# Bilinear sampling of a deformable convolution: five base values and sixteen clipped steps instead of twenty-one cell weights

## The chip, the cores and the metric

One core of one Trainium2 chip. The metric is the device time of one execution in microseconds, smaller is better. The kernel is written with explicit semaphores: every engine runs its own list of instructions in order and waits where the list says so.

## The reference, cut to what matters

Input x is (8, 64, 16, 16). Two residual layers follow each other, each on a group-normalised input. The first is a deformable attention: a 3x3 convolution gives, for each of 8 heads and 9 taps, an offset (dx, dy) and a weight; the values v are sampled bilinearly at the displaced place and summed over the taps.

```python
offsets = conv2d(x, off_w, off_b); aw = sigmoid(conv2d(x, attn_w, attn_b))
xp = (gx + 1.0) * 0.5 * (W - 1); yp = (gy + 1.0) * 0.5 * (H - 1)    # base grid + offset
x0 = floor(xp); y0 = floor(yp); x1 = x0 + 1; y1 = y0 + 1
sampled = corner(y0, x0, wy0*wx0) + corner(y0, x1, wy0*wx1) + corner(y1, x0, wy1*wx0) + corner(y1, x1, wy1*wx1)
head_out = einsum('nhckxy,nhkxy->nhcxy', sampled, aw)                # 9 taps
x = x + einsum('oc,nchw->nohw', Wo, combined)
```

The second layer (two 3x3 branches with running maxima, a 3x3 convolution of their sum, a 1x1 branch, two group norms, a last 3x3 convolution) is the same in both kernels.

## The kernel before

**The sampling as a window.** Instead of gathering, the kernel takes all cells of a window around each point. A partition is one (row y, image n) pair, 128 in all; the free axis runs over tap k, column x and head h. For a displacement d in cells the hat max(0, 1 - |u - d|) is the bilinear weight. Rows dy = -1, 0, 1 have five cells in x (d = -2 to 2), rows dy = -2 and 2 have three, 21 together (`DX`, `CELL0`, `CELLS`). A test (`vmin`, `vfar_sum`, `window_test`) looks whether any displacement leaves the window; a slow path, not taken with these inputs, covers that.

**Chunks.** The 16 columns go through in five chunks of 2, 4, 4, 4 and 2 columns (`CHUNKS`). For each chunk:

- TensorE makes the offsets, one column at a time: `conv_column`, 15 tap matmuls and one for the bias (L982, L990, L992).
- ScalarE copies them to `u` (`copy_offsets`), makes the modulation `mod` (L467), five distances |u - d| for x and y at once (L471, `distances`) and turns them to hats (L481, `hats`).
- VectorE makes `wy` = y hat times modulation (L777), a window check `edge`, then five products `prod` = x hat times `wy`, one for each row (L742), and sums the three cells of its own row over the nine taps by itself (L794, `cell`).
- TensorE sums the other 18 cells over the taps by nine transposes accumulated in PSUM, in three groups (`tap_sum`, L1009; 5 blocks of up to 128 columns in a chunk of four columns, 3 in a chunk of two); ScalarE copies each group back (`copy_sums`, L489) and TensorE transposes it again (`cells_back`, L1022).
- VectorE multiplies the weights with the shifted values, five `apply` instructions (L769) into a ring of three buffers `part` (`PARTS`); TensorE sums them by transposes (`row_sum`, L1034) and so frees a buffer (`part_used`). ScalarE evacuates (`evacuate`), TensorE projects (`y0`, L1045), VectorE adds the residual of the chunk before (`residual`, L688) between two applies.

Some `conv_column`s of later chunks stand on TensorE between these steps, by hand: `BEFORE` = (0, 1, 2, 0, 0) ahead of `tap_sum`, `BETWEEN` = (3, 2, 2, 0, 0) one ahead of each of the first `row_sum`s. Warm-up matmuls on constants stand ahead of `tap_sum` of chunks 3 and 4 (`WARM_CHUNK`).

**The start.** VectorE and ScalarE spread the normalised image and split it in a rounded and a rest part, in three ranges of columns (`RANGES`): VectorE casts to `g_pair` (L718) and subtracts to `g_cross` (L720); ScalarE copies both to the upper partitions (`copy_high`, L429 and L430). Chunk 0's convolution needs range 0 alone. ScalarE does `copy_high(2)` ahead of `copy_offsets(0)`. TensorE does chunk 0, two columns of chunk 1, then the values (`values`, 32 matmuls, L959, which need all three ranges), then the rest of chunk 1. GpSimd clears `wp_s` (L388) as soon as `w_split` is 2, which VectorE's L724 gives.

**The shifted values.** ScalarE copies the values from PSUM to `v[:, WIN]` (L441), and four DMAs on SP's queue shift them by -2, -1, 1 and 2 rows into the other rows of `v` (L327), in the order in which the applies use them.

Of the kernel before, what the change touches and what calls it, by code (L numbers as in the profile page):

```python
# [27 lines left out]
ALU = mybir.AluOpType  # L28
# [8 lines left out]
K2 = KS * KS  # L37
# [64 lines left out]
def build(nc, x, consts, w_off, w_v, off_bias, w_o, w12, b12, wp, wc1, wc2, vecs, out):  # L102
    with ExitStack() as ctx:
# [9 lines left out]
        x_t = sb("x_t", [C, N, HW])  # L113
# [10 lines left out]
        beyond = sb("beyond", [P, 2 * CKM])  # L124
        hat = sb("hat", [P, 2, ND, 2 * CKM])
        wy = sb("wy", [P, ND, CKM])
        prod = sb("prod", [P, CELLS * CKM])
        cell_t = sb("cell_t", [P, 5, P])
        cell = sb("cell", [P, 3, CXM])
        v = sb("v", [P, ND, W + 2 * WIN, C])  # L130
# [12 lines left out]

        vfar = part[:, :, :, :].rearrange("p b d s -> p (b d s)")[:, 0:VW * C].rearrange("p (x c) -> p x c", c=C)
# [35 lines left out]
        r12 = x_t[:, 0:HALF, :].rearrange("p (b r) q -> p b r q", b=2)  # L180
        maxima = x_t[:, HALF:N, :].rearrange("p (b r) q -> p b r q", b=2)
# [40 lines left out]
        v_moved = [sem(f"v_moved{i}") for i in range(ND)]  # L222
        off_ps = sem("off_ps")
# [5 lines left out]
        hat_used = sem("hat_used")  # L229
# [60 lines left out]
        def cell_blocks(c, g):  # L290
            q0, q1, _ = GROUPS[g]
            cols = (q1 - q0) * CHUNKS[c][1] * HEADS
            n = -(-cols // P)
            return n, cols // n, 2 * g, bank[(2, 3, 2)[g]]

        def cells_ps(c, i):
            cx = CHUNKS[c][1] * HEADS
            if CELL0[i] >= GROUPS[-1][0]:
                return bank[3][:, 2 * P:2 * P + 3 * cx]
            return cell_bank[:, CELL0[i] * cx:(CELL0[i] + 5) * cx]  # L300
# [8 lines left out]
        def _(sp):  # L309
# [13 lines left out]
            sp.wait_ge(v_ready, 1)  # L323
            for i in (4, 1, 3, 0):
                d = (i - WIN) * N
                dst, src = (slice(0, P - d), slice(d, P)) if d > 0 else (slice(-d, P), slice(0, P + d))
                sp.dma_start(v[dst, i, WIN:WIN + W, :], v[src, WIN, WIN:WIN + W, :]).then_inc(v_moved[i], 16)  # L327
# [14 lines left out]
            with sp.If(count > 0):  # L342
# [6 lines left out]
                             v[:, WIN, WIN:WIN + W, :].rearrange("p x c -> p (x c)")).then_inc(far_v0, 16)  # L349
# [13 lines left out]
        def _(pool):  # L363
# [44 lines left out]
        def _(act):  # L408
# [28 lines left out]
            def copy_values():  # L437
                act.wait_ge(v_zero, 1)
                act.wait_ge(v_ps, 1)
                for b in range(4):  # L440
                    last = nc.scalar.activation(v[:, WIN, WIN + 4 * b:WIN + 4 * (b + 1), :],  # L441
                                                bank[4 + b][:, :].rearrange("p (x q) -> p x q", q=P)[:, :, 0:C],
                                                ACT.Copy)
                last.then_inc(v_ready, 1)
# [16 lines left out]
            def distances(c, d0, d1):  # L461
                x0, w = CHUNKS[c]
                ck = K2 * w * HEADS
                xs = slice(x0, x0 + w)
                act.wait_ge(u_ready, c + 1)
                if d0 == 0:
                    nc.scalar.activation(mod[:, :, xs, :], u[:, 2 * K2:, xs, :], ACT.Sigmoid).then_inc(mod_ready, 1)  # L467
                    if c >= 2:
                        act.wait_ge(hat_used, c - 1)
                for d in range(d0, d1):  # L470
                    nc.scalar.activation(  # L471
                        hat[:, c % 2, d, 0:2 * ck].rearrange("p (k x h) -> p k x h", x=w, h=HEADS),
                        u[:, 0:2 * K2, xs, :], ACT.Abs, bias=float(WIN - d), scale=STEP).then_inc(dist_done, 1)

            def hats(c):
# [749 lines left out]
```

## Time and profile before

| | us |
|---|---|
| median of 3 runs | 151.67 |
| lowest, highest | 150.72, 152.64 |
| span of the profiled execution | 149.2 |
| start-up to the first VectorE work of chunk 1 | 0 to 43.84 |
| chunks 1 to 4 and the last residual | 43.84 to 109.51 |
| second layer and the output | 109.51 to 149.2 |

The profile has a page (busy time of the engines, the span in 40 slices, the chain of work that ended last, groups of instructions) and a trace that can be asked for stretches. "busy" of a matmul is modelled and overlaps its neighbours, so for TensorE the distance from start to start is what counts. A record's length on VectorE or ScalarE overlaps the next one by some 0.08 us.

### The profile page before, as it was taken

To read this page: it belongs to the slowest core of one execution; us is meant where nothing else is said; L and a number is where in the kernel's file an instruction comes from. 1 tells how busy PE (TensorE), PEld (TensorE's weight loads), DVE (VectorE), ACT (ScalarE), POOL (GpSimd) and SP (SyncE) were. 2 spreads that over 40 slices of the span, in tenths; PEclk is the share of its full clock that TensorE was granted. 3 is DMA by queue.
4 is the path that set the end of the run, shared out by engine and by line. 5 is a ranking of instruction groups with operands and counts; after the bars stand their busy time and mean duration, and the time that the engine had idled before them with its cause. 6 is when DMAs were issued, how large, how long until landed. Compare 5 with 4: busy or idle time off the path is not lost.

```text
span 149.2 us, 3269 instructions
## 1 busy us (share of the span) xinstructions
PE 129.2 (87%) x1395; PEld 111.3 (75%) x1395; DVE 110.5 (74%) x198; ACT 57.4 (38%) x102; POOL 18.5 (12%) x27
## 2 busy tenths in 40 slices
PE   4966399999999899999999998899887999797790
PEld 3654399998898889999899896687655667465460
DVE  5429895095459999799998999998757297965701
ACT  3009539837950768007880128012030317021100
POOL 8941120000000000000018000000003001030100
PEclk9999659999999999999999999999999999999999
DMA  3980000009964000000000000000000000000033
GB/s 95 271 152 0 0 0 4 0 15 256 244 120 108 19 7 0 0 0 4 0 0 0 0 4 0 0 0 4 0 2 4 4 0 4 0 4 0 0 75 70
DMA packets 6672, 5.48 MB, mean 37 GB/s; under 512 B 4656, under 2 KB 5938, under 8 KB 6658
## 3 DMA queue, kind: packets, MB, share of 16 engines
q1 hardware_dynamic: 5986, 4.26, 12.0%
q10 hardware_dynamic: 672, 1.02, 2.7%
q8 instruction: 11, 0.18, 0.5%
q14 instruction: 3, 0.02, 0.1%
HBM read 2.85 MB, written 0.52 MB: 23 GB/s over the span
## 4 chain that ended last, share of the span: by engine, by line
PE 50%; DVE 25%; issue 9%; DMA 6%; ACT 5%; SPq 1%; POOL 1%; POOLq 0%; DVEq 0%
PE bank L990 10%; PE bank L1009 9%; PE bank L982 8%; PE bank L1034 7%; DVE prod L742 7%; DMA prod<-in_w_off 6%; DVE part L769 3%; DVE x_t L861 3%; PE bank L1164 3%; PE bank L1131 3%; PE bank L959 2%; DVE wy L777 2%; DVE pooled L867 2%; DVE bn L580 2%; PE bank L943 2%
## 5 line engine op out<-in xcount | busy, mean ns | idle before, releaser
L742 DVE TENSOR_TENSOR prod<-hat,wy 128x1440 f32<-128x1440 f32 (+3 forms) x25 | 27.3, 1159 | 0.0
L769 DVE TENSOR_TENSOR part<-v,bank 128x1280 f32<-128x1280 f32 (+3 forms) x20 | 21.7, 1109 | 7.1 <-PE bank L1034 3.5
L1009 PE MATMUL bank<-cst,prod 128*128 128x128 f32 (+3 forms) x189 | 22.3, 272 | 0.8 <-DVE prod L742 0.8
L1034 PE MATMUL bank<-cst,part 128*128 128x128 f32 x168 | 21.1, 274 | 1.8 <-DVE part L769 1.4
L1009 PEld LDWEIGHTS bank<-cst,prod 128*128 128x128 f32 (+3 forms) x189 | 20.7, 131 | 1.4 <-DVE prod L742 1.0
L1034 PEld LDWEIGHTS bank<-cst,part 128*128 128x128 f32 x168 | 18.3, 140 | 3.2 <-DVE part L769 3.0
L943 PE MATMUL bank<-ones_r 128*128 128x512 f32 x67 | 18.5, 428 | 2.1 <-POOL w_pair L370 2.1
L990 PE MATMUL bank<-w_cross,g_cross 128*128 128x216 f32 x144 | 19.9, 285 | 0.0
L990 PEld LDWEIGHTS bank<-w_cross,g_cross 128*128 128x128 f32 x144 | 18.6, 203 | 0.0
L982 PE MATMUL bank<-w_pair,g_pair 128*128 128x216 f32 x96 | 15.3, 301 | 3.7 <-ACT g_cross L430 3.7
L943 PEld LDWEIGHTS bank<-ones_r 128*128 128x128 f32 x67 | 13.3, 207 | 4.9 <-POOL w_pair L370 2.1
L982 PEld LDWEIGHTS bank<-w_pair,g_pair 128*128 128x128 f32 x96 | 13.1, 209 | 4.4 <-issue 4.3
L471 ACT ACTIVATE hat<-u 128x576 f32<-128x576 f32 (+1 forms) x25 | 13.7, 579 | 0.0
L377 POOL TENSOR_TENSOR ab<-ab,half_pow 128x2 f32<-128x2 f32 (+1 forms) x7 | 5.8, 834 | 55.7 <-DVE ab L604 53.5
L481 ACT ACTIVATE hat<-hat 128x2880 f32<-128x2880 f32 (+1 forms) x5 | 10.7, 2132 | 0.2
L777 DVE TENSOR_TENSOR wy<-hat,mod 128x1440 f32<-128x1440 f32 (+1 forms) x5 | 6.8, 1351 | 5.2 <-ACT hat L481 5.2
L489 ACT ACTIVATE cell_t<-bank 128x256 f32<-128x256 f32 (+5 forms) x15 | 4.7, 317 | 14.4 <-PE bank L1009 14.3
L1164 PE MATMUL bank<-g,wc_s 64*64 64x256 f32 x144 | 8.5, 379 | 2.0 <-DVE g L890 2.0
L456 ACT ACTIVATE u<-bank 128x432 f32<-128x432 f32 x7 | 3.4, 528 | 16.3 <-PE bank L992 16.3
L1151 PE MATMUL bank<-pooled,wp_s 64*64 64x256 f32 x144 | 8.6, 379 | 1.1 <-DVE pooled L867 1.1
L1164 PEld LDWEIGHTS bank<-g,wc_s 64*64 64x64 f32 x144 | 5.9, 132 | 4.2 <-ACT g L547 2.9
L1131 PE MATMUL bank<-g,w_s 64*32 64x256 f32 x288 | 8.5, 377 | 0.1
(101 smaller groups left out, 154.9 us busy)
## 6 DMA issues: line engine op xcount, KB each, us to landing
v<-v SPq DMA_DIRECT2D x2, 480.0 KB, 6.2
v<-v SPq DMA_DIRECT2D x2, 448.0 KB, 5.9
prod<-in_w_off ACTq DMA_DIRECT2D x1, 486.0 KB, 7.0
prod<-in_w_off SPq DMA_DIRECT2D x1, 486.0 KB, 8.8
w_s<-in_w SPq DMA_DIRECT2D x4, 72.0 KB, 4.4
wc_s<-in_wc SPq DMA_DIRECT2D x2, 144.0 KB, 3.4
wp_s<-in_wp SPq DMA_DIRECT2D x4, 72.0 KB, 2.5
x_b<-in_x SPq DMA_DIRECT2D x1, 256.0 KB, 4.9
```

Of the source, the lines that this page charges most:

```text
L471: nc.scalar.activation(hat[:, c % 2, d, 0:2 * ck].rearrange("p (k x h) -> p k x h", x=w, h=HEADS), u[:, 0:2 * K2, xs, :], ACT.Abs, bias=fl ...
L481: nc.scalar.activation(hat[:, c % 2, :, 0:2 * ck], hat[:, c % 2, :, 0:2 * ck], ACT.Relu, bias=1.0, scale=-1.0).then_inc(hat_ready, 1)
L742: return nc.vector.tensor_tensor(prod[:, 0:K2 * CELLS * cx].rearrange("p (k q s) -> p q k s", k=K2, s=cx)[:, q0:q0 + nd], hat[:, c % 2, d0 ...
L769: nc.vector.tensor_tensor(part[:, n % PARTS, 0:nd, 0:cv].rearrange("p d (q e) -> p d q e", e=HD), moved, weights.unsqueeze(3).to_broadcast ...
L777: made_wy = tick(nc.vector.tensor_tensor(wy[:, :, 0:ck].rearrange("p d (k q) -> p d k q", k=K2), hat[:, c % 2, :, ck:2 * ck].rearrange("p ...
L943: nc.tensor.matmul(ps.rearrange("p (a q) -> p a q", q=P), ones_r[:, :], ones_r[:, :].unsqueeze(1).to_broadcast([P, 4, P]), start=True, sto ...
L982: nc.tensor.matmul(column_ps(c, j), g_pair[:, x + 2 * single, ky:ky + H, :].rearrange("p y n -> p (y n)"), w_pair[:, t, :], start=(t == 0) ...
L990: nc.tensor.matmul(column_ps(c, j), g_cross[:, x + kx, ky:ky + H, :].rearrange("p y n -> p (y n)"), w_cross[:, t, :], start=False, stop=False)
L1009: last = nc.tensor.matmul(out_ps[0:size, b * P:(b + 1) * P], prod[:, at:at + size], ident, start=(b == 0 and t == 0), stop=(b == n - 1 and ...
L1034: last = nc.tensor.matmul(comb_bank[:, j * P:(j + 1) * P], part[:, n % PARTS, d, j * P:(j + 1) * P], ident, start=(m == 0 and d == 0 and j ...
L1131: last = nc.tensor.matmul(image(bank[R12_BANK[g] + r][cols, 0:HW]), w12_s[rows, t, b * CD:(b + 1) * CD], window(g1, rows, DUO * g + k, t), ...
L1164: last = nc.tensor.matmul(image(bank[OUT_BANK[g] + k][r * C:(r + 1) * C, 0:HW]), wc2_s[rows, t, :], window(g2, rows, DUO * g + r, t), star ...
```

## The change

For one row the hats h(-2) .. h(2) in x sum to one inside the window, so the sum over five cells of h(d) v(d) is written as v(-2) plus four clipped steps min(1, max(0, u - d)) times the column differences v(d+1) - v(d), d = -2 .. 1. In rows dy = -2 and 2 the base is v(-1) and there are two steps. In numbers for a chunk:

- The five y hats times modulation are the weights of the bases. They are written into `prod` (places 16 to 20) and not into `wy`, and VectorE sums all five over the taps (before: three cells).
- 16 products step times base (4, 4, 4, 2, 2 cells), before 21.
- TensorE's `tap_sum` has two groups of 8 cells, before 8, 7 and 3: in a chunk of four columns 4 blocks and not 5, in one of two columns 2 and not 3. `cells_back` and `copy_sums` follow.
- The applies: one with the five bases, then rows of 4, 4, 4 terms, then rows 3 and 4 (2 terms each) as two instructions into one buffer. 21 terms as before. The order of rows is dy = 0, -1, 1, -2, 2.
- ScalarE: one |u| for both axes (`dist`), four row distances, four clipped ramps in x, each with their second step; 13 instructions for a chunk and not 7, on as many elements. `copy_sums` stands at two places and not three.
- A new tensor `dv` of column differences: GpSimd clears it (5 x 19 x 64 elements, ahead of the clearing of `wp_s`), later subtracts in two pieces when the values are there, and SP shifts it by rows in two pieces of 8 and 9 columns, eight DMAs behind the four of `v` and ahead of the second layer's weights. The four of `v` carry 14 or 15 columns, not 16.
- The first apply of chunk 0 waits for all four shifted rows of `v`; the steps of chunk 0 for `dv`'s first piece, row by row.
- TensorE makes the values directly behind chunk 0, then all four columns of chunk 1. `y0(c - 1)` stands ahead of the last `cells_back`.
- `x_t` is gone; its later use lies in `v`.

The diff, cut to its core:

```diff
-DX = [1, 2, 2, 2, 1]
-GROUPS = ((0, 8, 2), (8, 15, 3), (15, 18, 4))
+STEPS_X = ((-2, 4), (-2, 4), (-2, 4), (-1, 2), (-1, 2))
+GROUPS = ((0, 8, 2), (8, 16, 5))
+TERMS = (5, 4, 4, 4, 4)
+VCOLS = W + 3
+D_PIECES = ((1, 9), (9, 18))
...
+        dv = sb("dv", [P, ND, VCOLS, C])
...
+            sp.wait_ge(v_ready, 4)
+            for i in range(1, ND):
+                dst, src = row_parts(i)
+                at = -BASES[i]
+                sp.dma_start(v[dst, i, at:W, :], v[src, 0, 2:2 + W - at, :]).then_inc(v_moved[i], 16)
+            sp.wait_ge(dv_zero, 1)
+            for k, (xa, xb) in enumerate(D_PIECES):
+                sp.wait_ge(dv_ready, k + 1)
+                for i in range(1, ND):
+                    dst, src = row_parts(i)
+                    sp.dma_start(dv[dst, i, xa:xb, :], dv[src, 0, xa:xb, :]).then_inc(dv_moved[k][i], 16)
...
             pool.wait_ge(w_split, 2)
+            nc.gpsimd.memset(dv[:, :, :, :], 0.0).then_inc(dv_zero, 1)
             nc.gpsimd.memset(wp_s[:, :, :, :], 0.0).then_inc(wp_zero, 1)
+            pool.wait_ge(v_zero, 1)
+            pool.wait_ge(dv_zero, 1)
+            for k, (xa, xb) in enumerate(((0, 9), (9, 18))):
+                pool.wait_ge(v_ready, 2 * (k + 1))
+                nc.gpsimd.tensor_tensor(dv[:, 0, xa:xb, :], v[:, 0, xa + 1:xb + 1, :], v[:, 0, xa:xb, :],
+                                        ALU.subtract).then_inc(dv_ready, 1)
...
             copy_high(2)
             copy_offsets(0)
-            distances(0, 0, ND)
-            hats(0)
+            sizes_and_modulation(0)
+            row_distances(0)
+            row_hats(0)
+            short_of(0)
+            steps_x(0)
             copy_values()
...
+                copy_sums(c, 0)
                 if c + 1 < NC:
-                    distances(c + 1, ND - 1, ND)
-                    hats(c + 1)
+                    row_distances(c + 1)
+                copy_sums(c, 1)
+                if c + 1 < NC:
+                    row_hats(c + 1)
+                    short_of(c + 1)
+                    steps_x(c + 1)
...
-                for i in ROWS[:-1]:
+                ve.wait_ge(hat_ready, 2 * c + 2)
+                for i in range(ND):
                     product(i).then_inc(prod_ready, 1)
...
+                base_sum = tick(nc.vector.tensor_reduce(
+                    cell[:, :, 0:cx], cells[:, bases].rearrange("p q k s -> p q s k"), AX_X, ALU.add))
+                apply_bases()
+                apply_steps((0,))
+                apply_steps((1,))
+                if c:
+                    residual(c - 1)
+                apply_steps((2,))
...
+                apply_steps((3, 4))
...
-            conv_column(1, 0)
-            conv_column(1, 1)
             values()
-            conv_column(1, 2)
-            conv_column(1, 3)
-            pe.wait_ge(v_ready, 1)
+            for j in range(CHUNKS[1][1]):
+                conv_column(1, j)
+            pe.wait_ge(v_ready, 4)
...
                 cells_back(c, 0)
-                tap_sum(c, 2)
-                cells_back(c, 1)
-                cells_back(c, 2)
                 if c:
                     y0(c - 1)
+                cells_back(c, 1)
```

## Rows read from the trace of the kernel before

**Rows 1.** Busy time by stretch: chunks 1, 2, 3, then 4 to last residual (start:end, length, engines)
```profile
43.84:61.80 17.96, 16.98 (x156) 16.43 (x156) 16.76 (x18) 8.74 (x15) 0.00 (x0) 1.00 0.14 32
61.80:79.90 18.10, 17.93 (x166) 17.46 (x165) 16.98 (x17) 9.27 (x16) 1.88 (x4) 1.00 0.00 1
79.90:96.92 17.02, 15.79 (x125) 13.90 (x124) 16.88 (x17) 5.24 (x13) 1.57 (x2) 1.00 0.00 1
96.92:109.51 12.59, 11.22 (x93) 9.31 (x92) 10.23 (x23) 1.48 (x5) 0.00 (x0) 1.00 0.01 2
```

**Rows 2.** Waits over the whole span: who for whom, total us, times, longest
```profile
DVE part L769 <- PE bank L1034: 3.5, 3, 1.5
```

**Rows 3.** Groups by form, VectorE: busy us, mean ns of one, idle before
```profile
L742 DVE TENSOR_TENSOR prod<-hat,wy 128x1440 f32<-128x1440 f32 x9 | 14.4, 1653 | 0.0
L769 DVE TENSOR_TENSOR part<-v,bank 128x1280 f32<-128x1280 f32 x9 | 13.1, 1479 | 0.0
...
L794 DVE TENSOR_REDUCE cell<-prod 128x96 f32<-128x864 f32 x3 | 5.1, 1694 | 0.1
...
L769 DVE TENSOR_TENSOR part<-v,bank 128x768 f32<-128x768 f32 x3 | 2.9, 950 | 2.0 <-PE bank L1034 2.0
...
L794 DVE TENSOR_REDUCE cell<-prod 128x48 f32<-128x432 f32 x2 | 1.8, 901 | 0.0
```

**Rows 4.** Timeline of TensorE in chunk 1: tap sums (start, us, xcount)
```profile
49.07 4.17 PE L1009 MATMUL bank<-cst,prod 128*128 128x128 f32 x36 [0.81 <-DVE prod L742]
```

**Rows 5.** The chain that ended last: chunk 0's end, the values, a column of the convolution
```profile
23.63 0.11 PE bank L992
...
27.31 3.53 PE bank L959 x32
...
65.51 0.67 PE bank L982 x6
66.18 1.01 PE bank L990 x9
```

**Rows 6.** Timeline of all engines, 15 to 26 us: casts, memset, what ScalarE waits for
```profile
15.28 0.53 DVE L718 CAST g_pair<-g_t 64x720 fp32r<-64x720 f32 x1 [0.47 <-ACT g_t L423]
...
19.44 1.40 DVE L718 CAST g_pair<-g_t 64x576 fp32r<-64x576 f32 x1
19.47 1.06 POOL L388 MEMSET wp_s<- 128x1152 f32 x1 [3.04 <-DVE w_cross L724]
...
21.55 0.82 DVE L718 CAST g_pair<-g_t 64x1296 fp32r<-64x1296 f32 x1
...
22.40 1.28 ACT L429 ACTIVATE g_pair<-g_pair 64x1296 fp32r<-64x1296 f32 x1 [0.28 <-DVE g_pair L718]
...
24.89 0.59 ACT L451 ACTIVATE u<-bank 128x216 f32<-128x216 f32 x2
```

**Rows 7.** Timeline of GpSimd: the clearing of v
```profile
1.99 5.44 POOL L371 MEMSET v<- 128x6400 f32 x1
```

**Rows 8.** Granted clock by stretches of 1 us (value ahead of the last two columns)
```profile
15.00:16.00 1.00, 0.00 (x0) 0.00 (x0) 0.69 (x2) 0.79 (x3) 0.20 (x1) 0.92 0.00 0
...
22.00:23.00 1.00, 1.00 (x8) 1.00 (x7) 0.97 (x2) 0.72 (x2) 0.00 (x0) 0.67 0.00 0
```

**Rows 9.** Timeline of TensorE: its first work behind the idle stretch
```profile
17.45 2.87 PE L982 MATMUL bank<-w_pair,g_pair 128*128 128x216 f32 x12 [3.75 <-ACT g_cross L430]
```

**Rows 10.** Timeline of ScalarE: distances and hats of chunk 0, the copies of the values
```profile
25.74 1.76 ACT L471 ACTIVATE hat<-u 128x288 f32<-128x288 f32 x5
...
28.10 1.41 ACT L481 ACTIVATE hat<-hat 128x1440 f32<-128x1440 f32 x1
30.94 1.22 ACT L441 ACTIVATE v<-bank 128x256 f32<-128x256 f32 x4 [1.43 <-PE bank L959]
```

**Rows 11.** The tile v: its four DMAs, ns to issue, first and last start; landing
```profile
L327 SPq DMA_DIRECT2D v<-v x4: 593/876/2054, 32.2 to 34.7; - x4
...
DMA to landing us min/median/max: 3.7/6.2/8.1
```

More of the change, by code:

```diff
@@ L222, in build @@
         v_moved = [sem(f"v_moved{i}") for i in range(ND)]
+        dv_zero = sem("dv_zero")
+        dv_ready = sem("dv_ready")
+        dv_moved = [[sem(f"dv_moved{i}_{k}") for i in range(ND)] for k in range(len(D_PIECES))]
         off_ps = sem("off_ps")
@@ L464, in distances, with sizes_and_modulation @@
+            def sizes_and_modulation(c):
+                x0, w = CHUNKS[c]
                 xs = slice(x0, x0 + w)
                 act.wait_ge(u_ready, c + 1)
[L466 to L473, printed above, removed]
@@ new lines, in sizes_and_modulation, with row_distances, short_of @@
+                if c >= 2:
+                    act.wait_ge(prod_ready, ND * (c - 1))
+            def row_distances(c):
+                for i in range(1, ND):
+                    nc.scalar.activation(functions(c, 1, i), displacement(c, 1), ACT.Abs, bias=-float(DYS[i]),
+                                         scale=STEP).then_inc(dist_done, 1)
+            def short_of(c):
+                for i in range(1, ND):
+                    nc.scalar.activation(functions(c, 0, i), displacement(c, 0), ACT.Relu, bias=float(i - 2),
+                                         scale=-STEP).then_inc(dist_done, 1)
@@ new lines, in apply_bases, with apply_steps @@
+                def apply_bases():
+                    if c == 0:
+                        ve.wait_ge(v_ready, 4)
+                        for i in range(1, ND):
+                            ve.wait_ge(v_moved[i], 16)
+                    to = next_part()
+                    ve.wait_ge(step, base_sum)
+                    weighted(to, v, 0, x0, ND, VCOLS * C, cell[:, :, 0:cx]).then_inc(part_ready, 1)
+                def apply_steps(rows):
+                    to = next_part()
+                    d = 0
+                    for i in rows:
+                        if c == 0 and i == 0:
+                            ve.wait_ge(dv_ready, len(D_PIECES))
+                        if i and c in (0, 2):
+                            ve.wait_ge(dv_moved[c // 2][i], 16)
+                        ve.wait_ge(cell_ps, len(GROUPS) * c + (1 if STEP0[i] < GROUPS[0][1] else 2))
+                        at, n = STEPS_X[i]
+                        last = weighted(to[:, d:d + n], dv, i, x0 + at + 2, n, C,
+                                        cells_ps(c, i).rearrange("p (d q) -> p d q", d=n))
+                        d += n
+                    last.then_inc(part_ready, 1)
@@ L798, in chunk @@
-                for m, i in enumerate(APPLY[:-1]):
-                    if c and m == ND - 2:
-                        residual(c - 1)
-                    apply(i)
+                base_sum = tick(nc.vector.tensor_reduce(
[6 more added lines that the diff above has]
+                apply_steps((2,))
```

163 lines of the change are left out of this document (75 added, 88 removed).

## The prediction

> **What bounds the kernel now.** I read first the busy time of the engines by stretch, cut where VectorE begins a chunk. In chunks 1 to 3 VectorE is busy 16.8, 17.0 and 16.9 us of 18.0, 18.1 and 17.0, and TensorE is as full in the first two [rows 1]. So neither alone sets the pace. The waits say how the two are tied: VectorE's idle time in an apply ends with a row sum, 3.5 us in three waits [rows 2]; the last apply of a chunk needs one of the three buffers back, and TensorE has convolution columns between the row sums. Then I read the lengths of single instructions: VectorE's by form [rows 3], TensorE's from its timeline and from the chain [rows 4, 5]. Last, because the change puts new work there, the start: the timelines of all engines from 15 to 26 us [rows 6], the granted clock and the DMAs that shift the values. There no engine is full; the chain goes through whoever is late.
>
> **The steady chunks: what they gain.** VectorE's products cost 1.653 us for 1440 elements (5 cells of 288) [rows 3] and follow each other 0.08 closer than their records. I take 1.04 ns an element, the slope between the two forms of the applies being alike: (1.479 - 0.950)/512 = 1.03 [rows 3]. 21 cells are 6.7 us in the trace's chunk, 16 cells 4608 x 1.04 = 4.8 plus 5 starts of 0.07, 5.15: 1.55 less. The sum over the taps grows from 3 cells to 5: 1.694 us for 864 elements and 0.901 for 432 [rows 3] make 1.84 ns an element, so 1440 cost 2.75, 1.05 more. The applies have the same 21 terms and one instruction more, 0.1. The base product writes as much as `wy` did; into the strided `prod`, as the products have always done. Net 0.4 less on VectorE, 16.9 to 16.5 or 16.7 with its small gaps. The reduction is the trap in the title: of the 1.55 saved, two thirds are given back.
>
> TensorE loses 9 of 45 tap transposes; 36 take 4.17 us with the tail of the last [rows 4], 0.11 each, so 1.0 less, one block of `cells_back` (0.1) and one handover through ScalarE (0.3) less. Row sums stay, transposes of the same shape and price; a column of the convolution is 0.67 + 1.01 + 0.11 for the bias = 1.8 [rows 5].
>
> The period is a loop over both: products ready; second tap sum 2.0; cells back and `y0` 0.8; column 1.8, row sum 1.1, column 1.8, row sum 0.9 (now a buffer is free); last apply 1.3; base product and check 2.0, products 5.15. Sum 16.85. VectorE's own sum is 16.7, so the loop sets it by little. Against 17.96 and 18.10 [rows 1] that gives 1.1 and 1.25 us. In chunk 3 no columns stand between, VectorE sets the end: 17.02 to 16.65, 0.4. Chunks 1 to 3 together: 2.75 less. In chunk 4, 9 of 27 transposes go (1.0), VectorE's products lose 0.8 and the reduction adds 0.5; from its start to the last residual 12.59 [rows 1] becomes 11.65, 0.95 less. Steady part: **3.7 us less**.
>
> **The start: what the new clearing does.** GpSimd now clears `dv` at the moment at which it cleared `wp_s`, 19.47. `dv` has 6080 elements; `v` with 6400 took 5.44 us [rows 7], `wp_s` with 1152 took 1.06 [rows 6], so 0.83 ns an element and 5.17 us: 19.47 to 24.65. Beside it VectorE casts range 1 and range 2 of `g_pair`. The cast of 720 elements took 0.53 and that of 1296 took 0.82, without GpSimd; the one of 576, by that 0.45, took 1.40 and ended at 20.84, 0.3 behind the memset that ran beside it [rows 6]. So a cast does not run beside a memset of GpSimd; it stood for about the whole 0.95 that was left of it. I take the same with the long one: the cast of range 1 begins at 24.6 and ends at 25.0. Then GpSimd's `wp_s` runs and the cast of range 2 waits for it to 26.05 and ends at 26.8, before 22.37. If GpSimd's two memsets follow without a gap it is 27.6; if VectorE wins the first race, range 2 alone waits and ends at 25.9. Bounds of the delay: 3.5 to 5.2, I take 4.5, for it is the order that the trace shows.
>
> The Trainium skill, page "SBUF — State Buffer", section on the shared port, says that VectorE in a two-port mode (casts and copies) and GpSimd hold a common pair of ports exclusively, the loser standing for the whole instruction. The trace shows that for 1.06 us [rows 6] and can't show it for 5.17. By the page the delay is whole; if a wait were never longer than the 0.95 seen, it would be nothing beyond what is there, and that is my first rival.
>
> Who waits: ScalarE's `copy_high(2)` began at 22.40, on the cast, and `copy_offsets(0)` stands behind it, at 24.89 [rows 6]. Both move by 4.5: offsets copied from 29.35. Chunk 0's convolution is done at 23.7 [rows 5] and is not touched. But the values now stand directly behind it, and need `copy_high(2)`: TensorE has nothing from 23.7 to 29.35, 5.6 us, where before it had two columns of chunk 1 (3.6 us) as cover. The cover is gone.
>
> **The clock.** TensorE resumed at 17.45 from an idle time of 3.75 [rows 9], so it had worked to 13.7; the granted clock was 0.92 in the stretch 15 to 16 and 0.5 behind it [rows 8]: it fell to the lower level 2.2 us into the idle time. It came back at 22.3 (0.67 in 22 to 23), 4.9 us after the work resumed at 17.45; a matmul took 0.24 (12 in 2.87) [rows 9] where it takes 0.11 (6 in 0.67) [rows 5]. I expect the same for an idle time of 5.6: lower level at 26, and the values from 29.35 half as fast. They took 3.53 us [rows 5]; now 22 of 32 at 0.22 and 10 at 0.11, to 35.35.
>
> **ScalarE and the values.** Distances of 288 elements follow each other by 0.34 (5 in 1.76), the hats' 1440 elements took 1.41 [rows 10]. The new order, by these: |u| 0.35, four row distances of 144 elements 0.9, row hats 1.0, hence bases' weights ready 3.2 behind the offsets' start (before, all at 4.6); four ramps 0.9 and their second step 0.7, done at 4.75. Then the check 0.6: ScalarE is free at 34.7, so 0.7 before the values are. Copies 1.22 [rows 10]: `v_ready` at 36.65, before 32.16.
>
> **The DMAs.** The first shift landed 3.7 us behind its issue, at 35.9, the last at 34.7 + 8.1 = 42.8 [rows 11]: three of them, 1408 KB, in 6.9 us, 204 KB/us. Now v is 4 x 420 KB: first 40.3, last 46.5, and the first piece of `dv`, 928 KB, by 51.0. The bases wait for all of v, 46.5 to 47.3; rows 0 to 2 to 49.4. GpSimd's subtractions (576 elements each; from a memset's 0.6 to a few us) lie between 36 and 46 and are hidden either way.
>
> **Chunk 0 on TensorE.** Columns of chunk 1 4 x 1.8 to 42.5; tap sums to 44.5; ScalarE has `u` of chunk 1, |u|, and four row distances (1.5) ahead of the second copy: cells back at 46.6 (that is 1.3 us of waiting which no form of before has). Column, row sum, column, row sum: 51.2. Only then is the buffer for rows 3 and 4 free; `dv` is there too. Two short applies, 0.8: VectorE starts chunk 1 at **52.0**, before 43.84: 8.2 later.
>
> **Sum.** +8.2 - 2.75 - 0.95 = **+4.5 us**. The second layer is unchanged, and so is what lies outside the span. The profiled execution has 149.2, so 153.7; the runs' median is 2.5 above it, so 151.67 + 4.5 = **156.2 us**, 3.0% slower.
>
> **Rivals.** (1) *No blocking* (or one of under 1 us): the steady gain wins. Then the values start at 24.9, `v_ready` 31.45, and VectorE starts chunk 1 at 45.0 (buffers) to 46.2 (`dv` landing at 45.8): 1.2 to 2.4 later, minus 3.7, is -1.3 to -2.5: 149.8 us, at the best 149.2. What decides is the length of the cast of range 1 or 2: under 1.5 us, this one. Against it stands the one long cast [rows 6]. (2) *Blocked, but the clock does not fall* in the idle time: values 2.4 earlier on TensorE, row sums of chunk 0 2.5 earlier, VectorE at 49.5: +2.0, 153.7 us. For it: nothing in the trace; against it [rows 8]. (3) *Blocked twice or DMAs slower*: the two memsets in one go (+0.7), the lower clock lasting into chunk 1's columns (up to +1.5) or `dv` rows late behind each other: 157.5 to 158.5. (4) *A real gain of over 2%*: rival 1 with the shifted rows of `dv` landing at the pace of the first transfer and VectorE's steady period down to its own 16.5: 148.3.
>
> **Chances.** Forecast 0.60, rival 1 0.12, rival 2 0.12, rival 3 0.11, rival 4 0.05. The forecast's own terms (4.5 by 3.5 to 5.2; half-speed time by a microsecond; period by 0.2 a chunk) spread it from 154.8 to 157.3. The range leaves out rivals 1 and 4 and the top of 3: 152.3 to 158.0. A measurement of this kernel tells about 2%, 3.0 us, from no change: slower is the forecast but its low edge, rival 3, and a little of 2: 0.68; within 2% 0.25; faster 0.07.
>
> **What would show it.** Right: a cast of `g_pair` of 4 to 6 us beside GpSimd's `dv` memset; TensorE idle from 23.7 to about 29; a granted clock of 0.5 there; VectorE's base product of chunk 1 at 52; chunk starts 16.8 apart; reductions of 2.75 and 16 cells in 5.2. Wrong: casts of under 1 us (rival 1), clock 1.0 throughout (rival 2), a wait of VectorE for the `dv` DMA that ends behind 51, or chunk starts still 18 apart.

## The result and the profile after

| | before | after |
|---|---|---|
| median, us | 151.39 (4 runs) | 159.98 (4 runs) |
| lowest, highest | 150.72, 152.64 | 159.81, 161.34 |
| span of the profiled execution | 149.2 | 157.9 |
| mean granted clock of it | 0.976 | 0.934 |

The ratio is 1.060, 95% interval 1.051 to 1.068: 8.6 us slower where 4.5 was forecast, and the time lies above the range.

The start-up, on all engines between 20 and 31 us, after (start, duration, engine, line, operation, what the engine waited for):

```profile
20.00 5.50 DVE L774 CAST g_pair<-g_t 64x576 fp32r<-64x576 f32 x1
20.03 5.17 POOL L408 MEMSET dv<- 128x6080 f32 x1 [3.03 <-DVE w_cross L780]
25.13 1.37 POOL L409 MEMSET wp_s<- 128x1152 f32 x1
...
26.21 0.97 DVE L774 CAST g_pair<-g_t 64x1296 fp32r<-64x1296 f32 x1
...
29.70 0.59 ACT L477 ACTIVATE u<-bank 128x216 f32<-128x216 f32 x2
29.82 0.45 PE L1028 MATMUL bank<-w_v_pair,g_pair 128*128 128x128 f32 x1 [4.96 <-ACT g_cross L457]
```

The cast of 576 elements takes 5.50 us where it took 1.40 [rows 6]; it is over 0.3 behind the clearing of `dv`. `copy_offsets(0)` starts 4.8 later than before [rows 6], and TensorE stands idle for 4.96 us ahead of the values. (The cast itself begins 0.56 later in this execution, behind a load that landed later.)

The clock in those stretches (sum of the stretch, busy time of each engine, granted clock, DMA share, GB/s), after:

```profile
26.00:27.00 1.00, 0.00 (x0) 0.00 (x0) 1.00 (x2) 0.79 (x2) 0.50 (x1) 1.00 0.00 0
27.00:28.00 1.00, 0.00 (x0) 0.00 (x0) 0.96 (x2) 0.78 (x1) 0.00 (x0) 0.90 0.00 0
28.00:30.00 2.00, 0.18 (x1) 0.21 (x2) 1.15 (x4) 1.98 (x4) 0.00 (x0) 0.50 0.00 0
30.00:40.00 10.00, 10.00 (x48) 10.00 (x49) 5.29 (x9) 5.99 (x21) 2.20 (x2) 0.50 0.03 7
40.00:41.00 1.00, 1.00 (x6) 1.00 (x6) 0.00 (x0) 0.00 (x0) 0.58 (x1) 0.50 0.94 172
41.00:42.00 1.00, 1.00 (x9) 1.00 (x8) 0.00 (x0) 0.00 (x0) 0.00 (x0) 0.77 0.93 298
```

It fell in the idle time as expected, 2.9 us into it, but it was back at full speed only at 41.5: 11.6 us after TensorE had resumed, with TensorE full all the while. All the values, the first column of chunk 1 and part of the second ran at half speed. The low stretch ahead of it lasted longer too: from the idle time before chunk 0's convolution the clock was back at 24.4, 6.4 us after the work resumed at 18.02 (before: 22.7, 5.2 us), and chunk 0's convolution ended at 24.9 and not at 23.7. TensorE in the columns, after:

```profile
36.68 1.55 PE L1051 MATMUL bank<-w_pair,g_pair 128*128 128x216 f32 x6
38.03 2.12 PE L1059 MATMUL bank<-w_cross,g_cross 128*128 128x216 f32 x9
...
40.16 1.45 PE L1051 MATMUL bank<-w_pair,g_pair 128*128 128x216 f32 x6
...
42.57 0.83 PE L1051 MATMUL bank<-w_pair,g_pair 128*128 128x216 f32 x6
...
46.15 2.02 PE L1078 MATMUL bank<-cst,prod 128*128 128x128 f32 x17
```

The first column takes 3.5 us (36.68 to 40.16), the second 2.4, the others 1.8; the tap sums begin at 46.15.

VectorE from the last work of chunk 0 on, after:

```profile
37.30 1.40 DVE L863 TENSOR_REDUCE cell<-prod 128x80 f32<-128x720 f32 x1
48.46 0.82 DVE L810 TENSOR_TENSOR part<-v,cell 128x640 f32<-128x640 f32 x1 [9.76 <-DMA v<-v]
49.20 1.28 DVE L810 TENSOR_TENSOR part<-dv,bank 128x512 f32<-128x512 f32 x2
52.77 0.69 DVE L810 TENSOR_TENSOR part<-dv,bank 128x512 f32<-128x512 f32 x1 [2.29 <-PE bank L1100]
54.98 0.75 DVE L810 TENSOR_TENSOR part<-dv,bank 128x256 f32<-128x256 f32 x2 [1.53 <-PE bank L1100]
55.65 1.65 DVE L848 TENSOR_TENSOR prod<-hat,mod 128x1440 f32<-128x1440 f32 x1
```

The last line is the start of chunk 1: 55.65, before 43.84 [rows 1], so 11.8 later. The largest wait by far, 9.76 us for the DMA of `v`, looks like the cause; an experiment below shows what it costs.

Between the starts of the chunks, after:

```profile
55.65:72.77 17.12, 16.24 (x149) 15.54 (x148) 16.28 (x19) 8.91 (x20) 0.00 (x0) 1.00 0.24 47
72.77:89.93 17.16, 16.87 (x156) 16.29 (x155) 16.50 (x18) 9.44 (x21) 2.00 (x4) 1.00 0.00 1
89.93:106.38 16.45, 14.62 (x111) 12.35 (x109) 16.35 (x19) 5.40 (x18) 1.46 (x2) 1.00 0.00 1
```

Chunks 1 to 3 take 50.73 us and took 53.08 [rows 1]: the sampling itself is 2.35 us faster, and chunk 4 is some 0.9 faster. So 11.8 - 2.35 - 0.9 = 8.6, which is what the times say (the spans: 8.7).

### The profile page after: what moved, and what is told of

It is laid out like the page before. It is cut to its first block, busy times and chain, and to the rows that moved or that the text cites. A ratio compares the mean times of both kernels' runs of the same rounds, so it can differ in the third digit from the quotient of the medians.

```text
span 157.9 us, 3217 instructions
## 1 busy us (share of the span) xinstructions
PE 131.6 (83%) x1345; PEld 112.5 (71%) x1345; DVE 112.6 (71%) x203; ACT 58.3 (37%) x127; POOL 26.4 (17%) x30
## 3 DMA queue, kind: packets, MB, share of 16 engines
q1 hardware_dynamic: 7038, 6.10, 17.3%
## 4 chain that ended last, share of the span: by engine, by line
PE 40%; DVE 35%; issue 9%; DMA 6%; ACT 6%; SPq 1%; POOL 1%; DVEq 1%; POOLq 0%
DVE prod L802 10%; PE bank L1059 7%; DMA prod<-in_w_off 6%; PE bank L1078 5%; DVE part L810 5%; PE bank L1051 5%; PE bank L1028 4%; DVE g_pair L774 4%; PE bank L1100 4%; DVE v L930 3%; PE bank L1226 3%; PE bank L1193 3%; DVE prod L848 2%; PE bank L1089 2%; DVE pooled L936 1%
## 5 line engine op out<-in xcount | busy, mean ns | idle before, releaser
L810 DVE TENSOR_TENSOR part<-dv,bank 128x512 f32<-128x512 f32 (+2 forms) x25 | 19.9, 832 | 5.1 <-PE bank L1100 5.1
L802 DVE TENSOR_TENSOR prod<-hat,prod 128x576 f32<-128x576 f32 (+2 forms) x25 | 21.3, 920 | 0.5 <-ACT hat L531 0.5
L1012 PE MATMUL bank<-ones_r 128*128 128x512 f32 x67 | 19.3, 443 | 2.2 <-POOL w_pair L390 2.1
L1059 PEld LDWEIGHTS bank<-w_cross,g_cross 128*128 128x128 f32 x144 | 20.2, 218 | 0.0
L1078 PE MATMUL bank<-cst,prod 128*128 128x128 f32 x144 | 17.3, 274 | 1.3 <-DVE prod L802 1.3
L1078 PEld LDWEIGHTS bank<-cst,prod 128*128 128x128 f32 x144 | 15.8, 140 | 2.5 <-DVE prod L802 2.2
L810 DVE TENSOR_TENSOR part<-v,cell 128x1280 f32<-128x1280 f32 (+1 forms) x5 | 6.1, 1225 | 10.2 <-DMA v<-v 9.8
L863 DVE TENSOR_REDUCE cell<-prod 128x160 f32<-128x1440 f32 (+1 forms) x5 | 10.9, 2189 | 0.0
L1028 PE MATMUL bank<-w_v_pair,g_pair 128*128 128x128 f32 x16 | 6.7, 417 | 5.0 <-ACT g_cross L457 5.0
L848 DVE TENSOR_TENSOR prod<-hat,mod 128x1440 f32<-128x1440 f32 (+1 forms) x5 | 6.8, 1353 | 3.7 <-ACT hat L525 3.7
L1028 PEld LDWEIGHTS bank<-w_v_pair,g_pair 128*128 128x128 f32 x16 | 5.3, 331 | 5.1 <-DVE w_v_cross L785 5.1
```

Source lines behind the costliest of these rows:

```text
L802: return nc.vector.tensor_tensor(cells[:, STEP0[i]:STEP0[i] + n], hat[:, c % 2, at + 3:at + 3 + n, 0:ck].rearrange("p d (k s) -> p d k s", ...
L810: return nc.vector.tensor_tensor(to.rearrange("p d (q e) -> p d q e", e=HD), moved, weights.unsqueeze(3).to_broadcast([P, n, cx, HD]), ALU ...
L848: made_bases = tick(nc.vector.tensor_tensor(cells[:, bases], hat[:, c % 2, :, ck:2 * ck].rearrange("p d (k s) -> p d k s", s=cx), mod[:, : ...
L863: base_sum = tick(nc.vector.tensor_reduce(cell[:, :, 0:cx], cells[:, bases].rearrange("p q k s -> p q s k"), AX_X, ALU.add))
L1012: nc.tensor.matmul(ps.rearrange("p (a q) -> p a q", q=P), ones_r[:, :], ones_r[:, :].unsqueeze(1).to_broadcast([P, 4, P]), start=True, sto ...
L1028: last = nc.tensor.matmul(bank[4 + x // 4][:, (x % 4) * P:(x % 4 + 1) * P].rearrange("p (a c) -> p a c", c=C), src[:, x + 1, 1:H + 1, :].r ...
```

## The experiments

The kernels are built on the one after, unless said otherwise. Times are medians; before, on the same chips, was 151.2 to 151.7.

### What the clearing costs

**Cleared late.** `dv` is cleared behind `wp_s`, once VectorE's last split is done.

```diff
-            nc.gpsimd.memset(dv[:, :, :, :], 0.0).then_inc(dv_zero, 1)
             nc.gpsimd.memset(wp_s[:, :, :, :], 0.0).then_inc(wp_zero, 1)
+            pool.wait_ge(w_pair_ready, 3)
+            nc.gpsimd.memset(dv[:, :, :, :], 0.0).then_inc(dv_zero, 1)
```

> The changed kernel with one move on GpSimd: dv is cleared behind wp_s and only when VectorE has given w_pair_ready 3, its last cast of the start. Theory A (the common port: the 5.17 us clearing holds VectorE's cast of range 1, and all that follows from it, the lower clock too, makes the loss): the cast of 576 elements is back at 1.4 us (beside wp_s), TensorE idle between chunk 0 and the values for 1.2 us and not 5, granted clock 1.0 from 23 us on, chunk 1 begins on VectorE at 45.5 to 47, the time is 149.5 to 151.5 us, a ratio to the kernel before of 0.985 to 1.0. Theory B (the loss is of the new order on TensorE and of the twelve shifting DMAs, the clearing is beside it): chunk 1 begins behind 51 and the time stays over 155 us.

154.8 us (153.3 to 155.2), ratio 1.021 (1.014 to 1.027). The casts and the clearings in it:

```profile
19.59 1.40 DVE L775 CAST g_pair<-g_t 64x576 fp32r<-64x576 f32 x1
21.69 0.82 DVE L775 CAST g_pair<-g_t 64x1296 fp32r<-64x1296 f32 x1
...
19.61 1.06 POOL L408 MEMSET wp_s<- 128x1152 f32 x1 [3.04 <-DVE w_cross L781]
24.57 5.17 POOL L410 MEMSET dv<- 128x6080 f32 x1 [3.89 <-DVE w_v_cross L786]
```

The same memset of 5.17 us, moved to where VectorE has no cast, gives back 5.2 us of the 8.6. But 149.5 to 151.5 was expected. The clock was not at 1.0 from 23 us on; by slices of 3.8 us, with VectorE's bases and its start of chunk 1:

```profile
PEclk9999955557999999999999999999999999999999
...
43.33 0.83 DVE L811 TENSOR_TENSOR part<-v,cell 128x640 f32<-128x640 f32 x1 [9.27 <-DMA v<-v]
...
50.78 1.65 DVE L849 TENSOR_TENSOR prod<-hat,mod 128x1440 f32<-128x1440 f32 x1
```

It was at the lower level from 19.3 to 36.4, although TensorE stood idle for only 0.53 and 0.87 us in that time, and the values took 6.9 us here too. So the slow values do not need the idle time of 5 us, and the 5.2 us, between two kernels that both have them, are the price of the blocked cast.

**A clearing put into the kernel before.** GpSimd clears 3840 elements of `part` (for nothing but the time it takes) ahead of `wp_s`; VectorE waits for it behind its last split.

```diff
             pool.wait_ge(w_split, 2)
+            nc.gpsimd.memset(part[:, :, :, :], 0.0).then_inc(extra_clear, 1)
             nc.gpsimd.memset(wp_s[:, :, :, :], 0.0).then_inc(wp_zero, 1)
...
+            ve.wait_ge(extra_clear, 1)
```

> The kernel before, with one clearing more on GpSimd at the place where the changed kernel clears dv: the buffers part, 3840 elements, 3.2 us by 0.83 ns an element (dv itself finds no room in this kernel); VectorE waits for it long after. It computes the same. Theory A (the common port alone): the cast of 576 elements takes 3.6 us and not 1.4, or 4.6 if both clearings go ahead of it; ScalarE's offsets of chunk 0 come 2.2 to 3.2 us later, and the time is 153.5 to 155.5 us, more if the clock stays low behind the idle time that TensorE gets. Theory B: the clearing costs nothing, 151 to 152 us.

154.9 us (152.0 to 155.6; four runs too far apart for an interval).

```profile
20.00 4.63 DVE L720 CAST g_pair<-g_t 64x576 fp32r<-64x576 f32 x1
...
20.03 3.30 POOL L389 MEMSET part<- 128x3840 f32 x1 [3.04 <-DVE w_cross L726]
23.27 1.06 POOL L390 MEMSET wp_s<- 128x1152 f32 x1
```

One cast stands for both memsets back to back, 4.4 us. With none of the new sampling chunk 1 begins 4.5 later (48.36), of which 0.6 was there before the cast began. So a clearing alone makes the start late. Its size in the time is less sure: three runs are 2.7 to 4.1 us above the median before, and one, 151.95, is within 0.4 and has no trace.

### What the order of the values and the clock cost

**Columns ahead of the values**, as before the change.

```diff
+            conv_column(1, 0)
+            conv_column(1, 1)
             values()
-            for j in range(CHUNKS[1][1]):
-                conv_column(1, j)
+            conv_column(1, 2)
+            conv_column(1, 3)
```

> The changed kernel with TensorE's order of before: two columns of chunk 1 stand ahead of the values again, the clearing of dv stays where it is. The columns need range 1 alone, so they can begin at 26.8 and fill the idle time up to the values. Theory A: the cast stays at 5.5 us, ScalarE's offsets stay at 29.7. If the clock falls only in the long idle time, an idle time of 2.1 us keeps it at 1.0, values end at 34, chunk 1 begins at 51 to 52.5, time 155.5 to 157. If it falls here too, all stays at 159 to 160. Theory B's order part alone: the time falls to 152.

160.4 us (159.6 to 162.5), ratio 1.058 (1.052 to 1.063): nothing, in either direction. TensorE's idle time is 2.25 us and not 5, but the values come later by the columns and the bases wait to 48.34. Whether a short idle time keeps the clock up was not tested by it: the clock had fallen at 18.8, ahead of that idle time, and was back at 32.5.

**Both together.**

> The changed kernel with both: dv cleared late and two columns of chunk 1 ahead of the values. Theory A: no idle time of TensorE between 18 and 40 us, clock 1.0, steady gain in full: v is ready later than with the values first (32.2 against 31.5), chunk 1 on VectorE at 45.5 to 47, time 149.5 to 151 us, within 0.7 us of the kernel with the clearing late alone. Theory B: over 153.

154.9 us (153.7 to 156.1), ratio 1.022 (1.015 to 1.029), as with the late clearing alone, although the clock is 1.0 in the values and the columns are done at 35.3 and not at 41.3. The bases still wait for the DMA, to 43.80, TensorE stands idle behind them for 3.4 us, and chunk 1 starts at 50.00. So the lower clock of the late clearing cost nothing while `v` landed this late. Both kernels missed what was expected of them if the blocked cast made the loss, 149.5 to 151.5 us.

**Warm-up products in the gap.** 20 of them (0.23 us each) between chunk 0 and the values; the clearing stays early.

```diff
+            keep_warm(20, bank[0][:, :])
             values()
```

> The changed kernel with 20 warm-up matmuls on constants (4.7 us) in TensorE's idle time behind chunk 0. Nothing is earlier for any other engine; only the clock can differ. Theory A with the clock's part as large as the trace makes it (values 6.9 us instead of 3.5, two columns 3.5 us longer than they should): clock 1.0 from 25 us on, values 29.8 to 33.4, columns of chunk 1 done at 40.6 instead of 46.2, chunk 1 begins at 51 to 52.5 instead of 55.7, time 155.5 to 157 us. If the clock matters nothing on the path (the DMAs of v land as late anyway, at 48): 159 us or more.

Four runs, on two levels: 155.8 and 157.6, and twice 161.9, with a mean clock of 0.978 and 0.967 in the first two and 0.947 in the others. The profiled one is that of 157.6. Its clock by slices, and VectorE's start of chunk 1:

```profile
PEclk9999956999999999999999999999997899999999
...
51.43 1.65 DVE L848 TENSOR_TENSOR prod<-hat,mod 128x1440 f32<-128x1440 f32 x1
```

Here the clock is up in the values, and chunk 1 starts 4.2 earlier than after (51.43, not 55.65), although the cast took 6.50 us, 1.0 longer: in this execution VectorE did not get in between the two memsets. There is a second low stretch this time, between the layers (118.7 to 121.7 us, slice 31 and 32 of the clock row), which costs some of that again. The two runs at 161.9 have no trace.

**Both idle times covered**: 15 more warm-ups ahead of chunk 0, 24 in the gap.

```diff
-WARM_LOAD, WARM_START, WARM_CHUNK = 14, 18, (0, 0, 0, 16, 10)
+WARM_LOAD, WARM_START, WARM_CHUNK = 14, 33, (0, 0, 0, 16, 10)
...
+            keep_warm(24, bank[0][:, :])
             values()
```

> The changed kernel as it is, with 15 more warm-up products ahead of the first convolution and 24 between the convolutions of chunk 0 and the values (0.23 us each at full clock), so that TensorE is never idle for long in the start; the clearing and the transfers stay. If the lower clock behind the blocked cast is worth what one look with 20 warm-ups gave (chunk 1 at 51.4 where the changed kernel has 55.7), the time is 154.5 to 156.5 and the runs lie close together. If the lower clock costs little because the transfers of v end the wait anyway: 159 to 160.

159.9 us (158.3 to 161.5), ratio 1.050 (1.041 to 1.059). I had miscounted the cover: chunk 0 now ended at 22.0, the warm-ups at 27.6, the cast again took 6.5, and 2.6 us of idle time were left. TensorE around it:

```profile
21.98 5.64 PE L1012 MATMUL bank<-ones_r 128*128 128x512 f32 x24
30.24 0.30 PE L1028 MATMUL bank<-w_v_pair,g_pair 128*128 128x128 f32 x1 [2.62 <-ACT g_cross L457]
...
31.05 0.34 PE L1028 MATMUL bank<-w_v_cross,g_cross 128*128 128x128 f32 x1
31.19 0.42 PE L1028 MATMUL bank<-w_v_pair,g_pair 128*128 128x128 f32 x1
```

The clock fell at 31.1, that is 0.9 us after work had resumed, and stayed low for 10.2 us. Chunk 1 starts at 55.41. Against the execution with 20 warm-ups (the same cast of 6.5, the same transfers, the clock up) that is 4.0 us. The kernel after against that execution gives 4.2, plus 1.0 for its shorter cast, less 0.3 for its later start: 4.9. So the lower clock behind the blocked cast costs 4 to 5 us. That comes out of single executions: the covers did not keep the clock up reliably, and the medians of the two covered kernels, 159.7 and 159.9, are that of the kernel after.

### What the transfers of v cost

**The first chunks' part of v alone goes first.** Columns 0 to 5 are shifted at once, the rest behind the first piece of `dv`; chunk 2 waits for it. With late clearing and columns first, as in "both together".

```diff
-                sp.dma_start(v[dst, i, at:W, :], v[src, 0, 2:2 + W - at, :]).then_inc(v_moved[i], 16)
+                sp.dma_start(v[dst, i, at:V_SPLIT, :], v[src, 0, 2:2 + V_SPLIT - at, :]).then_inc(v_moved[i], 16)
...
+                for i in range(1, ND):
+                    if k:
+                        dst, src = row_parts(i)
+                        at = -BASES[i]
+                        sp.dma_start(v[dst, i, V_SPLIT:W, :], v[src, 0, 2 + V_SPLIT - at:2 + W - at, :]).then_inc(v_rest[i], 16)
...
+                    if c == 2:
+                        for i in range(1, ND):
+                            ve.wait_ge(v_rest[i], 16)
```

> The changed kernel with both moves, and v shifted in two pieces as dv is: the columns up to 5, which chunks 0 and 1 need, first (some 520 KB instead of 1680), then dv's first piece, then the rest of v and of dv, for which chunk 2 waits. The bases stay first. Theory C: bases at 39.5 to 40.5, no idle time of TensorE over 1.5 us in chunk 0, dv's first piece by 43.5, chunk 1 begins at 44.8 to 46, time 149.5 to 150.7 us: the steady gain of some 3 us shows for the first time against the kernel before. Theory D: the same bytes and four DMAs more to issue, chunk 1 behind 48, 153 us or more.

**148.8 us** (148.4 to 150.1), ratio 0.983 (0.976 to 0.990): faster than the kernel before, by 1.0 to 2.4%.

```profile
38.42 0.82 DVE L818 TENSOR_TENSOR part<-v,cell 128x640 f32<-128x640 f32 x1 [4.75 <-DMA v<-v]
39.16 1.37 DVE L818 TENSOR_TENSOR part<-dv,bank 128x512 f32<-128x512 f32 x2
41.93 0.69 DVE L818 TENSOR_TENSOR part<-dv,bank 128x512 f32<-128x512 f32 x1 [1.39 <-PE bank L1111]
44.15 0.75 DVE L818 TENSOR_TENSOR part<-dv,bank 128x256 f32<-128x256 f32 x2 [1.53 <-PE bank L1111]
44.82 1.65 DVE L859 TENSOR_TENSOR prod<-hat,mod 128x1440 f32<-128x1440 f32 x1
```

The bases start at 38.42, not 43.80, and chunk 1 5.2 us earlier; 6.1 us by the times. The idle time of TensorE behind the bases, and the low clock that came with it at 45 to 48 us, are gone too. Chunks 1 to 3 take 50.73 us here as in the kernel after, and chunk 4 is 0.8 faster than before; the start is 1.0 later than before (44.82 against 43.84), which leaves the 2.2 us by which the span is shorter.

**The same pieces in the kernel after**, with the early clearing and the values first.

> The changed kernel with v shifted in two pieces, so that chunks 0 and 1 wait for the first only; dv is still cleared early and the values still stand directly behind the convolutions of chunk 0. If the whole-row transfers of v are what bounds the start by themselves, the saving seen between the kernels with whole rows and with pieces (6.1 us) comes here too: about 154. If the clearing and TensorE's lower clock set the end of chunk 0 as well (in the changed kernel columns at 46.3, bases at 48.5, so that the transfers were only about 2 us behind the columns), it saves 2 us at most: 158 to 160. My theory is the second.

160.0 us (159.5 to 161.0), ratio 1.060 (1.054 to 1.066): nothing at all.

```profile
42.95 0.82 DVE L817 TENSOR_TENSOR part<-v,cell 128x640 f32<-128x640 f32 x1 [4.73 <-DMA v<-v]
48.69 1.29 DVE L817 TENSOR_TENSOR part<-dv,bank 128x512 f32<-128x512 f32 x2 [4.92 <-PE bank L1099]
52.45 0.69 DVE L817 TENSOR_TENSOR part<-dv,bank 128x512 f32<-128x512 f32 x1 [2.47 <-PE bank L1110]
54.66 0.75 DVE L817 TENSOR_TENSOR part<-dv,bank 128x256 f32<-128x256 f32 x2 [1.53 <-PE bank L1110]
55.33 1.65 DVE L858 TENSOR_TENSOR prod<-hat,mod 128x1440 f32<-128x1440 f32 x1
```

The wait for the DMA has lost 5 us, and a wait of 4.92 for TensorE's `cells_back` (L1099) stands in its place: the columns, in part at half speed, end at 45.8. The longest wait of the profile after was worth nothing while TensorE was that late, and 6.1 us where the columns were done at 35.3.

**Own row first** (whole rows of `v`, late clearing, columns first): in chunk 0 the steps of row 0, which need no transfer, stand ahead of the bases.

```diff
-                apply_bases()
-                apply_steps((0,))
+                if c:
+                    apply_bases()
+                    apply_steps((0,))
+                else:
+                    apply_steps((0,))
+                    apply_bases()
...
-                w, nd = CHUNKS[c][1], TERMS[m]
+                w, nd = CHUNKS[c][1], (TERMS if c else (4, 5, 4, 4, 4))[m]
```

> The changed kernel with both moves (dv cleared late, two columns of chunk 1 ahead of the values) and one more: in chunk 0 the steps of the own row, which need no DMA, are applied ahead of the bases, which wait for all four shifted rows. In the kernel with both moves the bases came at 43.8, TensorE stood from 41.3 to 44.7 for them and its clock fell. Theory C (what is left of the loss is that wait and the idle time behind it): the first row sum at 41, the clock stays, bases at 43.8 to 44.6, chunk 1 begins at 46.5 to 47.5 and not at 50.0, time 151.0 to 152.5 us. Theory D (the amount of data moved is the limit, the order is nothing): chunk 1 at 49 or later, 154 to 155 us.

153.3 us (151.9 to 158.0, ten runs), ratio 1.011 (1.006 to 1.016). By the medians 1.6 us of the 6.1 come from what is queued behind the waiting bases, by the start of chunk 1 in the two profiled executions (46.91 and 50.00) 3.1 of 5.2; the rest came only with the shorter transfers.

### What is left in the start

**Copy order.** On top of the pieces: in chunk 0 `copy_sums(0, 1)` ahead of the row distances of chunk 1.

```diff
                 copy_sums(c, 0)
+                if c == 0:
+                    copy_sums(c, 1)
                 if c + 1 < NC:
                     row_distances(c + 1)
-                copy_sums(c, 1)
+                if c:
+                    copy_sums(c, 1)
```

> The same as the kernel with v in pieces, and in chunk 0 ScalarE copies the second group of sums ahead of the four row distances of chunk 1 (TensorE waited 1.2 us for that copy in all variants). Expected: cells back 1.2 us earlier, chunk 1 begins 0.5 to 1.2 us earlier if TensorE's row sums set its start, nothing if the last dv row does; 148.5 to 150.5 us.

148.0 us (146.6 to 150.3), ratio 0.973 (0.966 to 0.980). 0.8 by the medians, with overlapping runs: likely, not shown.

**Values first, with pieces and late clearing.**

> The changed kernel with dv cleared late and v in two pieces; unlike the 148.8 us version the values stand directly behind the convolutions of chunk 0, as in the changed kernel. If the short idle of TensorE at 24 us before the values lets the lower clock stay until about 36, as in the run with the late clearing alone, the columns come at 41.4 and chunk 1 starts at about 48 to 50: 151.5 to 154. If the order of the two makes no difference once the transfers are short: 148.8.

151.7 us, and again two levels: 149.0 and 149.6, and 153.8 and 154.5 with a mean clock of 0.944 (the ratio, 0.989 with 0.982 to 0.995, is that of the lower two). The profiled one is of the first (chunk 1 at 45.10). At the upper level the order costs at most 0.8 us against 148.8; why two runs had the lower clock is not shown.

Beside the late clearing alone, which differs only in the whole rows of `v`, this shows what the pieces are worth. At a mean clock of 0.942 to 0.944 the times are 154.7 to 155.2 without pieces and 153.8 and 154.5 with them; at 0.966 it is 153.3 without, and at 0.974 and 0.988 149.0 and 149.6 with them. Slow values and late rows of `v` stand side by side and end at about the same time: with whole rows the clock was worth nothing ("both together"), at the lower clock the pieces are worth about 1 us, and only without both do 4 to 6 us come back. The runs are few, and those at 153.8 and 154.5 have no trace.

**The same with 5 warm-ups** between chunk 0 and the values.

> As the kernel before it in this list, with 5 warm-up products put between the convolutions of chunk 0 and the values, where TensorE stood idle for 0.9 us. If it is the clock in the values that costs the time, the cover brings back 148.5 to 150. If it is the order of values and columns, it stays where the run without the cover is, within 0.5.

150.6 us (149.5 to 151.1), ratio 0.996 (0.991 to 1.002). None of the four runs is at 154; by four runs against two of four that speaks for the clock as the cause, without proving it. Three of them lie 0.8 us and more above the lower two of the kernel without the warm-ups, which is not explained.

**The start covered**: the version with copy order and 15 more warm-ups ahead of chunk 0's convolution.

> The version with pieces and copy order of 148.0 us, with 15 more warm-up products ahead of the first convolution, where TensorE stood idle from 13.7 to 17.4. If that idle is what keeps chunk 0's convolutions at the lower clock (12 at 0.24 us), they end about 1.4 us earlier and the first values with them: 146.5 to 147.5 and fewer runs with a low mean clock. If the clock falls there for another reason, 148.0 with the same spread.

**146.6 us** (146.2 to 148.6), ratio 0.970 (0.965 to 0.975), the best of all. And the same 15 warm-ups in the kernel before:

> The kernel before, with the same 15 warm-up products more ahead of the first convolution. If what they brought the version with pieces (148.0 to 146.6) is a matter of the start alone and the same in either sampling, it is 149.5 to 150.5 here. If in the kernel before the start is bound by VectorE's and ScalarE's work and not by TensorE, the time stays within 0.4 of 151.4.

149.9 us (149.3 to 151.7, ten runs), ratio 0.991 (0.987 to 0.996). So about 1.4 us of the gain is this cover, which either sampling can have; set against each other with the cover in both, the ratio is 0.970/0.991 = 0.978. That is not the sampling alone: the shifts in pieces and the copy order were never given to the kernel before, in which VectorE too waits 2.0 us in two waits for the DMAs of `v`. What the trace ties to the sampling are the 2.35 us of chunks 1 to 3 and the 0.9 of chunk 4.

## Why the prediction was right in kind and wrong in size

- **Steady chunks**: forecast -2.75, measured -2.35; chunk 4 -0.95 against about -0.9. The products of the steps took 5.23 (forecast 5.15), the reduction 2.72 (2.75), the period 17.12 and 17.16 (16.85): 0.45 us too hopeful. The gain stays in the version in pieces, with the same 50.73 us for chunks 1 to 3. That its 148.8 us lies close to what rivals 1 and 4 gave for a start without blocking (149.8 and 148.3) is luck: they are about whole rows of `v`, and the two kernels with whole rows and no blocked cast took 154.8 and 154.9.
- **The blocked cast**: right in length, place, order and in who waits. `copy_offsets(0)` came 4.81 later, 4.25 without the later start of that execution; 4.5 was forecast. Two other kernels' executions took the other order, with a cast of 6.5 (the bound's upper side). Chunk 0's convolution, which was not to be touched, ended 1.1 later, 0.6 of it by its later start and the rest by the clock. Rival 1, no blocking, is out, and by the late clearing the block is worth 5.2 us of time. The Trainium skill, page "SBUF — State Buffer", section "Who interferes with whom", has the loser stand for the whole instruction; 5.50 us beside a memset of 5.17 agrees.
- **The clock: the step that failed.** It fell as forecast, so rival 2 is out, but the prediction took one recovery, 4.9 us after the work resumed [rows 8, 9], for a constant ("I expect the same"). (Even that one was 5.2: 0.67 in the stretch from 22 to 23 means that the lower level held to 22.7, not 22.3.) It came back after 11.6. The values took 6.9 us and not 6.0; the columns of chunk 1, put at full speed (7.2 us), took 9.5. Columns done: forecast 42.5, measured 46.15; of these 3.65 the later start of the values (29.82, forecast 29.35) has 0.5, the values 0.9, the columns 2.3. From there everything ran as forecast, late by the same amount: cells back 50.06 (46.6), chunk 1 at 55.65 (52.0). Rival 3 named "the lower clock lasting into chunk 1's columns" and gave it at most 1.5; rival 2 priced the clock at 2.5 in all where the pairs of runs give 4 to 5.
- **The DMAs**: all of `v` landed at 48.4, forecast 46.5; `v_ready` was late by 1.5 of that. It was said that they do not set the end of chunk 0 but the buffers do, and the pieces alone confirm it: 0 us. What the prediction did not see is that they stand close behind, and rival 1 put them too low: it had chunk 1 at 45.0 to 46.2, set by the buffers or by `dv`, if the cast is not blocked. The two kernels of that kind have it at 50.78 and 50.00, behind bases that wait for `v` to 43.33 and 43.80 (one had the lower clock, the other the columns first, so neither is rival 1 to the letter). With TensorE on time the shorter transfers are worth 6.1.
- **The sum**: 3.65 at the start of chunk 1 and 0.45 in the steady part are the 4.1 between forecast (+4.5) and time (+8.6).
- **The range** ended at 158.0 because the clock, a state of the chip and not a duration, was given the spread of a duration: a microsecond around one observation.

## What to carry to other kernels

Put a long GpSimd memset where VectorE has nothing to cast: here the cast stood for the memset's whole length. The length of a wait in the profile is not what it costs: shorten it and look what stands behind. Two delays that end at the same time hide each other, so an edit that removes one of them and gains nothing does not clear it. And when work moves so that TensorE goes idle, price the work behind it twice, with a short return of the clock and with a long one, rather than take one recovery as the rule.

## What was not expected of the hardware

- The return of the clock varies: 5.2 us after the resumption before the change, 11.6 after it, 11.1 in the kernel with both covers. In that one it fell 0.9 us after TensorE had resumed from 2.6 us of idle time. After the same idle time of 3.6 us ahead of chunk 0's convolution, the lower level lasted 3.4 us in the kernel with the own row first (17.3 to 20.7) and 17.1 us in the one cleared late (19.3 to 36.4). What decides this is not shown. The same kernel's executions differ (155.8 to 161.9 with 20 warm-ups; 149.0 to 154.5 with the values first), and the mean clock differs with them.
- In the kernel with copy order, chunk 0's products take 5.28 us for 5 of 576 elements while GpSimd subtracts (5.28 to 5.30 in six kernels), and 2.83 where it does not:

```profile
30.32 5.28 DVE L813 TENSOR_TENSOR prod<-hat,prod 128x576 f32<-128x576 f32 x5 [0.50 <-ACT hat L539]
...
31.35 3.56 POOL L422 TENSOR_TENSOR dv<-v 128x576 f32<-128x576 f32 x2 [1.19 <-ACT v L476]
```

GpSimd's own two subtractions take 3.56 there and 2.78 in the kernel after, where VectorE is mostly idle. A memset did not slow VectorE's subtraction to `g_cross` (576 elements, 0.75 us beside the memset of `wp_s` in the kernel after, 0.75 without one before), only its casts. What decides this was not tried.
